# Attention pipeline with shorter lags: products seven and nine chunks behind the scores, and a batch's output projected three chunks after its last product with V

## What is computed

```python
xn = layernorm(x)
Q, K, V = xn @ Wq.T, ctx @ Wk.T, ctx @ Wv.T           # 16 heads of 16 columns
scores = where(causal, Q @ K.T, -inf) / sqrt(16)
x = x + tanh(g_xattn) * ((softmax(scores) @ V) @ Wo.T + bo)
logits = layernorm(x) @ controller + ramp             # groups of 32 rows, 128 expert slots
perm = (logits == max(logits over the group's rows))
x = x + tanh(g_ffn) * combine(perm, relu(dispatch(perm, layernorm(x)) @ f1 + bias) @ f2)
```

## Time and profile before

| | |
|---|---|
| median of 3 runs | 292.98 us (292.14 to 294.31) |
| the profiled execution | 291.55 us, of which its span is 289.8 us |
| PE busy | 239.9 us, 83% |
| DVE busy | 204.4 us, 71% |
| ACT busy | 172.6 us, 60% |
| POOL busy | 128.8 us, 44% |

### The profile page before, as it was taken

One profiled execution on the slowest core, in us unless ns is written; L12 is line 12 of the kernel. 1 busy time (PEld: TensorE's weight loads), 2 busy tenths in 40 slices (PEclk: granted clock), 3 DMA queues, 4 the chain that ended last, 5 costly groups with the idle time before them and its releaser, 6 DMA issues.

```text
span 289.8 us, 7624 instructions
## 1 busy us (share of the span) xinstructions
PE 239.9 (83%) x2914; PEld 190.6 (66%) x2914; DVE 204.4 (71%) x446; ACT 172.6 (60%) x361; POOL 128.8 (44%) x243
## 2 busy tenths in 40 slices
PE   0638495997897997979988878589998999989995
PEld 0527393776675876867766655467776888877773
DVE  4985758599996895957777799899995555522222
ACT  3433667577587686855766646267775545455552
POOL 5652445647776678762756656525544000000000
PEclk9996869799999999998999999999999999999999
DMA  7855679442434342242200000089910000001222
GB/s 204 192 149 147 183 187 267 115 113 58 133 104 129 96 112 78 74 129 58 56 4 6 4 4 1 12 308 392 387 67 2 1 2 2 2 20 60 69 72 72
DMA packets 27237, 29.52 MB, mean 102 GB/s; under 512 B 3459, under 2 KB 22595, under 8 KB 27203
## 3 DMA queue, kind: packets, MB, share of 16 engines
q1 hardware_dynamic: 26771, 28.46, 33.1%
q10 hardware_dynamic: 432, 0.59, 0.9%
HBM read 14.06 MB, written 2.10 MB: 56 GB/s over the span
## 4 chain that ended last, share of the span: by engine, by line
PE 31%; DVE 20%; POOL 20%; issue 17%; ACT 5%; SPq 3%; DMA 3%; ACTq 0%; POOLq 0%; DVEq 0%
POOL pT L410 8%; PE banks L817 8%; PE banks L789 6%; PE banks L771 6%; PE banks L826 3%; DVE rsum L1155 3%; PE banks L526 2%; SPq L269 2%; DVE permb L1200 2%; POOL xs L404 2%; POOL qp L387 2%; POOL onl L434 2%; DMA w<-in_wattn_dram 2%; DVE xn L1100 2%; PE banks L635 2%
## 5 line engine op out<-in xcount | busy, mean ns | idle before, releaser
L1147 DVE TENSOR_REDUCE nmax<-banks 128x4 f32<-128x512 f32 x64 | 43.7, 683 | 29.3 <-PE banks L589 29.3
L410 POOL TENSOR_SCALAR_AFFINE_SELECT pT<-pT 128x512 f32<-128x512 f32 x64 | 41.0, 642 | 47.2 <-ACT pT L917 47.1
L922 ACT ACTIVATE banks<-cb 128x512 f32<-128x512 bf16 x62 | 37.0, 596 | 9.8 <-DVE nmax L1147 9.7
L917 ACT ACTIVATE pT<-banks 128x512 f32<-128x512 f32 x64 | 37.5, 589 | 8.8 <-PE banks L606 8.3
L606 PE MATMUL banks<-qst,kst 99*128 99x128 bf16 x256 | 25.9, 225 | 4.3 <-DMA qst<-nT 3.6
L635 PE MATMUL banks<-pT,va 128*32 128x128 f32 x512 | 27.7, 289 | 0.8 <-POOL pT L410 0.8
L1155 DVE RECIPROCAL rsum<-banks 128x256 f32<-128x256 f32 x16 | 28.0, 1747 | 0.0
L589 PE MATMUL banks<-kst,qst 96*128 96x128 bf16 x256 | 26.2, 227 | 1.9 <-ACT banks L922 1.6
L635 PE MATMUL banks<-pT,ones 128*32 128x128 f32 x512 | 26.2, 277 | 0.0
L1042 ACT ACTIVATE ys<-banks 128x1024 f32<-128x1024 f32 x16 | 16.7, 1047 | 14.3 <-PE banks L817 14.2
L1334 DVE SCALAR_TENSOR_TENSOR xs<-banks,tg,xs 128x256 f32<-128x256 f32 x16 | 7.7, 484 | 24.5 <-PE banks L826 24.5
(11 more groups left out here) (120 smaller groups left out, 643.3 us busy)
## 6 DMA issues: line engine op xcount, KB each, us to landing
wx<-in_wexp_dram SPq DMA_DIRECT2D x32, 256.5 KB, 7.3
kst<-kp SPq DMA_DIRECT2D x48, 128.0 KB, 2.5
qst<-qp SPq DMA_DIRECT2D x48, 128.0 KB, 2.4
cT<-in_ctxT_dram SPq DMA_DIRECT2D x8, 256.0 KB, 3.5
out_dram<-xs SPq DMA_DIRECT2D x16, 128.0 KB, 1.7
xs<-in_x_dram SPq DMA_DIRECT2D x3, 512.0 KB, 4.1
xs<-in_x_dram SPq DMA_DIRECT2D x2, 256.0 KB, 3.8
w<-in_wattn_dram ACTq DMA_DIRECT2D x2, 256.0 KB, 5.0
```

The lines of the kernel that those rows point to most:

```text
L410: pool.affine_select(p, p, [[0, HC], [1, P]], ALU.is_ge, 0.0, base=0, channel_multiplier=-1)\
L917: act.activation(pT[:, n % PR, :], BT[n % 2], ACT.Exp, scale=float(D) ** -0.5).then_inc(p_ready, 1)
L922: act.activation(BS[n % 2], causal, ACT.Copy).then_inc(mask_placed, 1)
L1147: dve.tensor_reduce(nmax[:, b % 2, :].rearrange("p (e j o) -> p e o j", e=2, o=KH)[:, e, o], BS[n % 2].rearrange("p (j t) -> p j t", j=HC) ...
```

## The change

`LT` goes from 8 to 7 and `LA` from 10 to 9. In TensorE's slot `scores_less_max` moves behind `scores` and `spread_max`. `weigh_out` of batch b moves from slot 4b+14 to 4b+13, `out_high` from ahead of the exponentials of slot 4b+15 to behind those of 4b+14, `split_out` from 4b+16 to 4b+15, `project_out` from 4b+19 to 4b+15, and `residual` from the front of slot 4b+20 to behind the row maxima of 4b+16. The loop has four slots fewer. The split of Wo comes four slots earlier. The bounds on which `project_out` and `spread_max` wait for their shared bank follow the new order.

```diff
-LT = 8
-LA = 10
-SLOTS_N = 4 * NB + 17
+LT = 7
+LA = 9
+SLOTS_N = 4 * NB + 13
...
# GpSimd
-                if s % 4 == 0 and 0 <= n // 4 - 4 < NB:
-                    split_out(n // 4 - 4)
+                if s % 4 == 3 and 0 <= n // 4 - 3 < NB:
+                    split_out(n // 4 - 3)
...
-                if n == 16:
+                if n == 12:
                     weight_low(WO)
...
# TensorE
-                pe.wait_ge(v_ready, min(b + 4, NB))
+                pe.wait_ge(v_ready, min(b + 3, NB))
...
-                if b >= 4:
-                    pe.wait_ge(x1_ready, b - 3)
+                if b >= 3:
+                    pe.wait_ge(x1_ready, b - 2)
...
-                if 0 <= n - LT < CH:
...
-                    scores_less_max(n - LT)
                 if n < CH:
                     scores(n)
...
                     spread_max(n // 4 - 1)
+                if 0 <= n - LT < CH:
...
+                    scores_less_max(n - LT)
...
-                if s % 4 == 3 and 0 <= (n - 19) // 4 < NB:
-                    project_out((n - 19) // 4)
+                if s % 4 == 3 and 0 <= (n - 15) // 4 < NB:
+                    project_out((n - 15) // 4)
...
# ScalarE
-                if s % 4 == 3 and 0 <= n // 4 - 3 < NB:
-                    out_high(n // 4 - 3)
                 if 0 <= n - LT < CH:
                     exps(n - LT)
+                if s % 4 == 2 and 0 <= n // 4 - 3 < NB:
+                    out_high(n // 4 - 3)
...
-                if n == 15:
+                if n == 11:
                     weight_high(WO)
...
# VectorE
-                if s % 4 == 0 and 0 <= (n - 20) // 4 < NB:
-                    residual((n - 20) // 4)
                 if n < CH:
                     row_max(n)
+                if s % 4 == 0 and 0 <= (n - 16) // 4 < NB:
+                    residual((n - 16) // 4)
...
-                if s % 4 == 2 and 0 <= n // 4 - 3 < NB:
+                if s % 4 == 1 and 0 <= n // 4 - 3 < NB:
                     weigh_out(n // 4 - 3)
```

More of the change, by code:

```diff
@@ L684, in _ @@
                 s, g = n % 8, n // 8
-                if 0 <= n - LT < CH:
-                    if n == LT:
-                        pe.wait_ge(qr_ready, 2)
-                    scores_less_max(n - LT)
                 if n < CH:
@@ L696, in _ @@
                     spread_max(n // 4 - 1)
+                if 0 <= n - LT < CH:
+                    if n == LT:
+                        pe.wait_ge(qr_ready, 2)
+                    scores_less_max(n - LT)
                 if 0 <= n - LA < CH:
```

## The result

| | before | changed |
|---|---|---|
| median | 293.44 us (292.14 to 294.31) | 331.85 us (330.69 to 335.73) |
| ratio to before | | 1.131, 95% interval 1.125 to 1.136 |
| profiled execution, its span | 291.55, 289.8 us | 335.73, 334.0 us |
| mean granted clock over the span | 0.965 | 0.898 (0.906 to 0.917 in the other runs) |

The change makes the kernel 38 us slower. The profiled execution is the slowest of the five, 4 us above the median, with the lowest clock; pair times are read with that in mind.

What follows compares the result with a forecast made beforehand. The loop was taken as bounded by TensorE's own work. Terms 18.4 + 1.5 + 4.6 + 2.0 + 3 = 29.5 us on 291.55, plus 1.4 for the median, gave 322.5 us; range 305 to 334.

Steps and rivals of the forecast that it cites:

- The path of an output, first batch: First batch of a middle pair: rest of the output ready 9.4 us after slot 1's scores, TensorE waits 4.5 us.
- Second batch: Second batch of a middle pair: rest of the output ready at 7.05 us, TensorE there at 5.25, waits 1.8 us.
- What goes: TensorE's wait before transposing the maxima: all of its 1.5 us a pair disappears.
- A pair without the clock: Middle pair of batches, clock loss left out: 22.6 us instead of 17.8, 4.8 more.
- The last two pairs: Four batches without K, Q and x work: 8.7 us each, 1.15 more, together 4.6 us.
- The end of the loop: From the last scores to the first routing product: 26.1 us instead of 24.1, 2.0 more.
- The paths together: Output paths over loop and end, without the clock: 18.4, 1.5, 4.6 and 2.0 us more.
- TensorE's clock: Falls to half clock at TensorE's long waits: four falls of 0.7 us each, 3 us in all.
- Better overlap: Rival: engines catch up during TensorE's waits, first batch waits only 1.8 us; 308 us, chance 0.18 for 300 to 313.
- no wait: Rival: the output's rest is ready before TensorE reaches its projection, so the kernel is not slower; 283 us, chance 0.04.
- the forecast's band: Whole kernel: time from 313 to 332 us, given a chance of 0.62.
- the rival in which clock and paths add up: Rival: two clock falls a pair, longer end of loop, stretches lengthened by falls; 337 us, chance 0.12 for above 332.

Runs made afterwards that it cites:

- the outputs alone: Kernel of before with its lags and order, only the projection moved to slot 4b+16 and the residual to the front of 4b+17: 347.0 us, ratio 1.176.

## Why the prediction was right, and where it was off

The direction, the mechanism and the place of every large wait are as forecast; the time, 331.85 us, is in the range of 305 to 334 but near its end, 9 above the forecast of 322.5. The term for the clock is some 10 us too small, and that the time is still in the range is owed to the width of the range. Point by point:

- **The path of an output, first batch.** Worked out from the scores: `k_rest` 2.33, `onh` 5.2, exponentials 7.4, projection 9.4, wait 4.5. Measured 2.19, 5.04, 7.14, 9.28 and 4.26, since TensorE stood there at 5.0 and not at 4.88. That ScalarE's four instructions lie in it is shown by the run with only ScalarE's order changed.
- **Second batch.** 1.8 forecast; 1.67 to 1.91 measured.
- **What goes.** The wait for the maxima went as forecast. The prediction took it as given and did not look for what held it up; the run with the exponentials first shows that it was the rounding ahead of them.
- **A pair without the clock.** 22.6 forecast, 22.5 in the run with matmuls in the waits.
- **The last two pairs.** 8.7 a batch forecast. With the clock kept up it is 9.05 (from 165.08 to 174.13 between transposes of the maxima), without it some 10.2 (181.66 to 191.89). A part is a wait that I had not counted, for the transfer of the maxima, 0.2 to 0.7 us a batch: the product that needs it comes sooner than before.
- **The end of the loop.** 26.1 forecast, 27.9 measured.
- **The paths together.** 26.5 us forecast without the clock. In the run with matmuls in the waits the first routing product starts at 213.90, 25.9 us later than the 188.01 of before.
- **TensorE's clock: the term that was mis-sized.** I took 3 us, four falls of 0.7. Keeping TensorE busy in the waits is worth 13.5 us. Two things were wrong in that step. First, the price: the two pairs that gave 0.7 do not hold the same work. The one with the fall has 231 matmuls, the other 247. With the exponentials first the clock stays at 1.00, and the same two pairs, from projection to projection, are 16.2 and 14.9 us:

```profile
104.02:120.21 16.19, 16.19 (x250) 13.34 (x247) 13.48 (x22) 13.22 (x29) 12.92 (x23) 1.00 0.38 101
120.21:135.11 14.90, 14.40 (x235) 11.41 (x231) 12.07 (x18) 11.55 (x25) 10.73 (x21) 1.00 0.39 107
```

The second pair is 1.3 us shorter when nothing falls, so by these rows the fall went with 2.0 us and not 0.7 (TensorE's busy time for this pair is 16.1 in the trace of before and 14.4 here). Second, the number of falls. The loop of the changed kernel and then that of before:

```profile
60.00:235.00 175.00, 133.00 (x1715) 104.53 (x1713) 103.79 (x205) 84.65 (x184) 84.36 (x159) 0.86 0.19 52
60.00:190.00 130.00, 111.19 (x1674) 87.22 (x1672) 107.23 (x201) 84.05 (x181) 82.97 (x157) 0.99 0.25 66
```

Cut into stretches of half a microsecond, the first shows eleven falls to 0.50, some 48 us together, and the second shows one. Eleven falls for 13.5 us are 1.2 each, an estimate from the profiled execution, which is the slowest. The Trainium skill, TensorE: Matmul & The Clock Gate, Part 1, states that the array falls to half clock after it has been idle. The trace agrees: each of the eleven begins inside a wait of the projection or within 1 us behind it, and five of the sixteen waits, of 1.6 to 1.7 us, have none. The six falls and more that the prediction drew from that rule, at its price of 0.7, make some 4 us, 1 more than the term that I took: the rule at that price would not have mended the sum.
- **The rivals.** Better overlap (308) and no wait (283) are ruled out by sixteen waits. The measured time lies at the edge between the forecast's band (313 to 332) and the rival in which clock and paths add up (337), 9 from the one number and 5 from the other. That rival was nearer on the clock (8 us, and 6 for stretches lengthened by it, where 13.5 were measured); at the end of the loop the surplus over the forecast is 1.8 us, where it had 3.
- **A step left out.** I ascribed nothing to the lags as such. Alone they cost 12 us, through the queue behind the rounding; in the full change that wait does not exist, since the rounding no longer waits for the projection before it. The costs therefore don't add: 12 us for the lags alone and 52 for the outputs alone, 38 for the change. The run with the outputs alone is not the exact other half of it either, since its projection stands one slot later and rounding and rest keep their old places.

## What to carry to other kernels

When steps of a software pipeline move closer, lay the path of the moved result through every engine's written order, and count each instruction that stands between its steps; compare the sum with the work that the waiting engine has left, and do it for each kind of batch. Ask of each engine's list whether an instruction that waits for long stands ahead of one that others wait for: here one such swap, `onh` behind the exponentials, gave 3.5%, while the shorter lags gave nothing and cost some 4 us even with it. Add the clock to every periodic wait of TensorE, at a price taken from two stretches that hold the same work: compare the counts of instructions first.

## What was not expected of the hardware

- Waits of 2.5 to 2.9 us once a batch (the outputs alone) keep the mean granted clock of a middle pair at 0.83 to 0.84, as low as waits of 4.3 and 1.7 us in turn do (0.82). Filling them with unused matmuls raised it to 1.00 and made the kernel 15 us faster, and 13.5 us in the changed kernel: added work on the engine that bounds the loop shortened the time by 4%.
- The shorter lags alone lengthened TensorE's waits by little and still cost 12 us: 9.8 of the 12.2 us in the profiled executions are the same matmuls at a lower mean clock.
- With one swapped line the waits for the maxima between 60 and 200 us, 9.9 us in all, were gone and the kernel was 10 us faster, while TensorE's busy time stayed the same (239.9 and 239.6 us): on an engine that is busy 83% of the span, short waits counted in full.
